# Second layer norm's output and expert weights transposed through block transposes and a DRAM scratch, with three more pipeline stages and a reordered set-up

## The chip, the cores and the metric

The kernel runs on one core of one Trainium2 chip. The metric is the device time of one execution in microseconds (us), from the first to the last instruction. One core has five engines with instruction streams of their own: TensorE (PE; its weight loads are shown apart as PEld), VectorE (DVE), ScalarE (ACT), GpSimd (POOL) and SyncE (SP, which here only starts DMAs). They meet in semaphores. Everything is float32.

## What is computed

The input is 8 sequences of 2048 rows of 256 numbers. Two sublayers, each with a layer norm ahead, a layer norm behind and a residual sum:

```python
x = x + _layernorm(attn(_layernorm(x)))
x = x + _layernorm(ffn(_layernorm(x)))
```

The attention is causal and linear, in chunks of 128 rows, with a running state of 256x256 per sequence. The feed-forward part is the sum of a dense branch and a sparse one that picks 8 of 1024 experts for each of 4 heads:

```python
q = jnp.einsum('btd,ed->bte', hidden_states, W_q)
sim = jnp.einsum('pbthn,hkpn->pbthk', q, keys)
scores_xy, idx_xy = jax.lax.top_k(sim, K)
...
scores, pk = jax.lax.top_k(all_scores, K)
...
w = jax.nn.silu(jnp.einsum('btd,bthkd->bthk', hidden_states, de) * jax.nn.softmax(scores, axis=-1))
experts_states = jnp.einsum('bthk,bthkd->btd', w, ue)
dense = jnp.einsum('bti,di->btd', jax.nn.silu(jnp.einsum('btd,id->bti', hidden_states, W_up)), W_down)
return dense + experts_states
```

## The kernel before

The 16384 rows are 128 tiles of 128 rows, taken chunk by chunk with the 8 sequences in turn, so that tile t follows tile t-8 of its sequence. The kernel is written engine by engine. Each engine has a function `body(t, steady)`, and `pipeline(body)` calls it once per step; `t[k]` is the tile that entered k steps ago. A step handles several tiles at once, each at another stage (`STAGES = 10`). The order of the calls in a body is the order of the engine's instructions, written out by hand. Engines do not share a step's start: they wait for each other only by semaphores.

Gathering nothing, the kernel computes the experts densely: all 1024 products with `down_embed` (`deT`, in two halves of 512), a selection by threshold, and a product of 1024 expert weights with `up_embed` (`ue`).

One tile passes through these steps.

- DVE computes the first norm `xn1`. PE turns it (`turn`, two 128x128 transposes into PSUM), ACT copies it to `xn1T`, and PE forms v, q and k. ACT applies relu and exp to q and k, DVE joins them to `sig`. PE forms the masked scores, the memory product, the numerator and the state update (`ds_ps`, added to `state` by DVE). The result is `mix`, and after another norm `x_mid`.
- DVE computes the second norm `xn2` (line 765). PE turns it (line 587), ACT copies it out of PSUM into `xn2T` (line 639), laid out as [128, 2 buffers, 2 chunks, 128], each chunk contiguous. `xn2T[:, b, c, :]` is the stationary operand of the route product (`sc_ps`) and of the products with `deT` (`d_ps`), and the moving operand of the products with `wupT` (`u_ps`, 128 columns at a time).
- ACT copies the route scores (line 653). POOL adds them pairwise to `sums` for each head (`key_sums`, 128x1024). DVE finds the best eight, POOL forms candidates, DVE selects (`picked`), ACT takes the exponential (`prob`, lines 680 to 709), DVE multiplies, ACT applies Silu into `wexp` (lines 646 to 667).
- Two DMAs issued by POOL (lines 435 and 452) add the four heads of `wexp` together. DVE then transposes the 128x1024 sum in blocks of 32x32 (line 783). Its output pattern `turned_blocks` writes neighbouring elements 8 floats apart. SP stores the result to the DRAM scratch `w_way` (line 375) and reads it back by four DMAs into `gT`, [128, 2, 128, 8] (line 377), which finishes the transposition.
- PE multiplies `gT[:, b, :, c]` as the stationary operand, whose columns lie 8 floats apart, with `ue[:, c, :]` (line 584). The dense branch adds `hT` times `wdownT` into the same bank (line 557). After the last norm DVE forms `x_out`, and SP stores it.

The stationary reads that matter here:

```python
product(y_ps, IC, lambda c: hT[:, t[7] % 2, c, :], lambda c: wdownT[:, c, :], stop=False)
product(y_ps, EC, lambda c: gT[:, t[7] % 2, :, c], lambda c: ue[:, c, :], start=False)
```

In the set-up all weights are loaded by SP, transposed by PE in groups of four blocks (`turned`), evicted by ACT, and centred by DVE (`centre`). PE waits for all of it (`SET_ALL`, `CENT_ALL`) before its first step.

## Time and profile before

| | |
|---|---|
| median of 3 runs | 3030.0 us (3028.74 to 3034.31) |
| the profiled execution, its own time | 3034.47 us |
| its span, first to last instruction | 3032.7 us |
| mean granted TensorE clock | 0.992 |
| busy: PE, PEld | 2970.0 us, 2431.6 us |
| busy: DVE, ACT, POOL | 2420.2 us, 2532.4 us, 1955.8 us |

Busy time counts the compute instructions of an engine. A product in float32 shows as two matmul instructions in the trace, each with a weight load. The duration of a matmul in the trace contains its way through the array, so that neighbours overlap: what a matmul costs its engine is the distance from one start to the next, and this document reads blocks of matmuls from start to start. The same holds to a lesser degree of ACT and DVE, where neighbours overlap by some 0.1 us.

### The profile page before, as it was taken

The page shows a single profiled execution, that of the slowest core. Times are in us where ns is not written, and L with a number is a line of the kernel's source. Part 1 is how long each engine was busy: PE and PEld are TensorE (multiplying, and loading weights), DVE is VectorE, ACT ScalarE, POOL GpSimd, SP SyncE. Part 2 cuts the span into 40 slices and gives each one's busy share as a digit, 9 for nine tenths or more (in the row PEclk, how much of TensorE's full clock was granted, in tenths as well). Part 3 has the DMA queues.
Part 4 walks back from the last instruction along what each step waited for, and adds up shares of the span by engine and source line. Part 5 has one row for each costly group of instructions (what it writes and reads, how often), then busy time and mean ns, then how long its engine had stood idle before and what let it go on. Part 6 is the DMA issues. An engine that isn't in the chain of part 4 may idle for free.

```text
span 3032.7 us, 46880 instructions
## 1 busy us (share of the span) xinstructions
PE 2970.0 (98%) x15402; PEld 2431.6 (80%) x15402; DVE 2420.2 (80%) x5764; ACT 2532.4 (84%) x3854; POOL 1955.8 (64%) x2455
## 2 busy tenths in 40 slices
PE   6899999999999999999999999999999999999996
PEld 5678888888887888888888888888878888888875
DVE  3878888888887888888888788888878888888884
ACT  3888888888888888888888888888888888888884
POOL 2666666666666666666666666666666666666763
PEclk8999999999999999999999999999999999999998
DMA  3455555555555555555555555555555555555555
GB/s 96 96 130 128 122 126 129 125 125 127 129 124 129 127 126 124 127 126 124 131 129 124 122 131 123 129 126 128 124 129 127 125 124 128 125 124 130 129 124 120
DMA packets 188360, 378.33 MB, mean 125 GB/s; under 512 B 18899, under 2 KB 122324, under 8 KB 188116
## 3 DMA queue, kind: packets, MB, share of 16 engines
q0 software_dynamic: 53248, 201.34, 36.9%
q1 hardware_dynamic: 134868, 173.99, 18.3%
q8 instruction: 122, 2.00, 0.3%
q14 instruction: 122, 1.00, 0.1%
HBM read 90.05 MB, written 83.89 MB: 57 GB/s over the span
## 4 chain that ended last, share of the span: by engine, by line
PE 95%; DMA 2%; issue 1%; DVE 1%; POOL 1%; ACT 1%; SPq 0%; POOLq 0%; DVEq 0%
PE banks L529 86%; PE banks L547 3%; PE banks L534 2%; PE banks L608 2%; PE banks L601 1%; DMA wexp<-wexp 1%; DMA sums<-in_L_ffn_keys_dram 0%; SPq L353 0%; POOL sums L418 0%; DMA gT<-w_way 0%; DVE w_blocks L783 0%; PE banks L513 0%; POOL rstd L404 0%; PE banks L520 0%; PE banks L498 0%
## 5 line engine op out<-in xcount | busy, mean ns | idle before, releaser
L418 POOL TENSOR_TENSOR sums<-scores 128x1024 f32<-128x1024 f32 x512 | 1033.9, 2019 | 749.7 <-ACT scores L653 749.7
L404 POOL TENSOR_TENSOR rstd<-var_eps,minus_half 128x1 f32<-128x1 f32 x512 | 498.0, 1110 | 69.0 <-DVE var_eps L855 35.7
L529 PE MATMUL banks<-ue,gT 128*128 128x256 f32 x2048 | 528.9, 412 | 13.7 <-DMA gT<-w_way 13.7
L529 PEld LDWEIGHTS banks<-ue,gT 128*128 128x128 f32 x2048 | 502.7, 336 | 16.1 <-DMA gT<-w_way 14.5
L529 PE MATMUL banks<-xn2T,wupT 128*128 128x128 f32 x4096 | 498.8, 275 | 3.1 <-DVE state L821 3.1
L529 PEld LDWEIGHTS banks<-xn2T,wupT 128*128 128x128 f32 x4096 | 487.4, 192 | 10.1 <-DVE state L821 3.6
L529 PE MATMUL banks<-deT,xn2T 128*128 128x512 f32 x1024 | 481.3, 592 | 0.0
L529 PE MATMUL banks<-wdownT,hT 128*128 128x256 f32 x2048 | 465.0, 380 | 6.0 <-ACT y_sb L650 6.0
L529 PEld LDWEIGHTS banks<-wdownT,hT 128*128 128x128 f32 x2048 | 380.5, 191 | 54.2 <-issue 7.5
L529 PEld LDWEIGHTS banks<-deT,xn2T 128*128 128x128 f32 x1024 | 185.1, 190 | 130.8 <-issue 123.4
L783 DVE STREAM_TRANSPOSE w_blocks<-wexp 128x1024 f32<-128x1024 f32 x128 | 260.9, 2039 | 4.8 <-DMA wexp<-wexp 4.6
L529 PE MATMUL banks<-route,xn2T 128*128 128x512 f32 x512 | 243.5, 598 | 4.6 <-ACT xn2T L639 4.6
L811 DVE SCALAR_TENSOR_TENSOR picked<-sums,cand_best,banks 128x1024 f32<-128x1024 f32 x128 | 163.9, 1280 | 85.2 <-PE banks L529 85.0
L695 ACT ACTIVATE hT<-banks 128x512 f32<-128x512 f32 x128 | 76.4, 597 | 148.1 <-PE banks L529 148.1
L758 DVE SCALAR_TENSOR_TENSOR picked<-sums,cand_best,banks 128x1024 f32<-128x1024 f32 x128 | 163.9, 1280 | 35.5 <-POOL sums L418 35.5
L831 DVE SCALAR_TENSOR_TENSOR prob<-picked,rz,prob 128x1024 f32<-128x1024 f32 x128 | 191.2, 1494 | 0.0
L444 POOL TENSOR_TENSOR cprob<-cmask,cdif 128x112 f32<-128x112 f32 x128 | 59.2, 462 | 199.7 <-DVE cmask L842 199.7
L796 DVE TENSOR_SCALAR dens<-banks 128x2 f32<-128x2 f32 x128 | 20.5, 160 | 204.2 <-PE banks L608 204.2
L787 DVE MAX8 top<-scores 128x8 f32<-128x16 f32 x512 | 83.6, 163 | 116.5 <-ACT scores L653 116.2
L435 POOL DMA_DIRECT2D wexp<-wexp x128 | 158.4, 1237 | 27.9 <-issue 7.4
L695 ACT ACT_TABLE_LOAD x128 | 164.2, 1283 | 2.3
L635 ACT ACT_TABLE_LOAD x128 | 164.2, 1283 | 2.3
(135 smaller groups left out, 6695.9 us busy)
## 6 DMA issues: line engine op xcount, KB each, us to landing
wexp<-wexp POOLq DMA_DIRECT2D x128, 1024.0 KB, 8.0
wexp<-wexp POOLq DMA_DIRECT2D x128, 512.0 KB, 4.6
w_way<-w_blocks SPq DMA_DIRECT2D x128, 512.0 KB, 2.6
gT<-w_way SPq DMA_DIRECT2D x512, 128.0 KB, 3.0
x_in<-_attn_hidden_states_dram SPq DMA_DIRECT2D x128, 128.0 KB, 2.9
out_dram<-x_out SPq DMA_DIRECT2D x128, 128.0 KB, 1.7
wexp<-in_L_ffn_W_up_dram SPq DMA_DIRECT2D x1, 1024.0 KB, 8.3
prob<-in_L_ffn_down_embed_dram SPq DMA_DIRECT2D x1, 1024.0 KB, 10.9
```

The lines of the kernel that those rows point to most:

```text
L404: return nc.gpsimd.tensor_tensor(rstd[:, n, m:m + 1], var_eps[:, n, m:m + 1], minus_half[:, :], ALU.pow)
L418: return nc.gpsimd.tensor_tensor(sums[:, k, :, :], scores[:, k, 0:XIN].unsqueeze(2).broadcast_to([P, XIN, NKEYS]), scores[:, HEADS + k, :] ...
L435: pool.dma_start(wexp[:, 1::2, :], wexp[:, 0::2, :], accum_op=ALU.add).then_inc(s_head_pairs_summed, 16)
L529: last = nc.tensor.matmul(out, lhs(c), rhs(c), start=(start and c == 0), stop=(stop and c == chunks - 1))
L547: last = nc.tensor.matmul(ds_ps[:, c, :], sk_nat[:, c * P:(c + 1) * P], v_one[:, :], start=True, stop=True)
L635: nc.scalar.activation(z_last[:, :], z_last[:, :], ACT.Silu, scale=last_down[:, t[6] % 2:t[6] % 2 + 1], accum_out=w_last[:, t[6] % 2:t[6] ...
L695: nc.scalar.activation(flat(hT[:, t[5] % 2, 4:8, :]), u_ps[1][:, :], ACT.Silu).then_inc(s_hidden_1_ready, 1)
L758: nc.vector.scalar_tensor_tensor(picked[:, 0, :], head(sums, 2), best[:, 2, TOP - 1:TOP], down, ALU.is_ge, ALU.mult).then_inc(s_head_2_sel ...
L783: nc.vector.transpose(turned_blocks(w_blocks, EC), blocks(wexp[:, HEADS - 1, :])).then_inc(s_expert_weights_blocks_turned, 1)
L787: nc.vector.max(top[:, 0, k, :], scores[:, k, 0:XIN])
L811: nc.vector.scalar_tensor_tensor(picked[:, 0, :], head(sums, 0), best[:, 0, TOP - 1:TOP], down, ALU.is_ge, ALU.mult).then_inc(s_head_0_sel ...
L831: nc.vector.scalar_tensor_tensor(prob[:, 0, :], picked[:, 0, :], rz[:, t[5] % 2, 0:1], prob[:, 0, :], ALU.mult, ALU.mult).then_inc(s_head_ ...
```

## The change

- `xn2T` gets the layout [128, 2 buffers, 128, 2 chunks]. PE and ACT no longer make it. DVE transposes `xn2` in blocks of 32x32 into `xn2_blocks`, SP stores that to a DRAM scratch `xn2_way` and reads it back by four DMAs. PE then reads `xn2T[:, b, :, c]`, neighbouring elements 2 floats apart, as stationary operand (route, `deT`) and as moving operand (`wupT`).
- DVE writes `w_blocks` contiguously. The four DMAs read it back into `g_parts`, and a new ACT instruction copies `g_parts` into `gT`, now [128, 2, 8, 128], with contiguous stationary operands.
- `STAGES` goes from 10 to 13. The y products run on `t[10]` rather than `t[7]`, the products with `xn2T` on `t[7]` and `t[6]` rather than `t[5]` and `t[4]`. `hT` gets three buffers, `x_mid` ten slots. The bodies of all engines are written in another order.
- In the set-up, x of tile 0, the keys and `W_rq` are loaded ahead of `ue`, `de_in` and `wdown_in`. The transposes of `down_embed` and `W_down` (`LATE`, 8 groups) are moved into PE's and ACT's first attention step. Centring `ue` and `wdownT` is moved into DVE's steps.

The core of the diff:

```diff
-        xn2T = sb("xn2T", [P, 2, DC, P])
+        xn2T = sb("xn2T", [P, 2, P, DC])
...
+        xn2_blocks = sb("xn2_blocks", [P, D])
+        xn2_way = nc.dram_tensor("xn2_way", [2, P, D], fp32).ap()
...
-        gT = sb("gT", [P, 2, P, EC])
+        gT = sb("gT", [P, 2, EC, P])
+        g_parts = sb("g_parts", [P, BLOCKS, EC, BLOCK])
...
-        STAGES = 10
+        STAGES = 13
...
+            sp.dma_start(x_in[:, 0, :], x_tiles[:, chunk_of(0), seq_of(0), :]).then_inc(s_x_loaded, 16)
+            sp.dma_start(wup_in[:, :, :], W_up.rearrange("(c p) n -> p c n", p=P)).then_inc(s_w_up, 16)
+            sp.dma_start(keys_in[:, :, :, :], keys.rearrange("h k s n -> k h s n")).then_inc(s_w_route, 16)
...
+                if t[9] is not None:
+                    sp.wait_ge(s_expert_weights_blocks_turned, t[9] + 1)
+                    sp.dma_start(w_way[t[9] % 2, :, :], w_blocks[:, :]).then_inc(s_expert_weights_blocks_out[t[9] % 2], 16)
...
+                if t[6] is not None:
+                    sp.wait_ge(s_xn2_blocks_turned, t[6] + 1)
+                    sp.dma_start(xn2_way[t[6] % 2, :, :], xn2_blocks[:, :]).then_inc(s_xn2_blocks_out[t[6] % 2], 16)
...
+                    gather(xn2T[:, t[6] % 2, :, :].rearrange('p (i t) c -> p i (t c)', t=BLOCK), xn2_way[t[6] % 2, :, :], s_xn2_blocks_in[t[6] % 2])
...
-                    turn(t_ps, xn2).then_inc(s_xn2T_in_psum, 1)
...
+                    if t[5] == 0:
+                        late(range(len(parts)))
...
+                    moved(pe, s_xn2_blocks_in, t[6], BLOCKS)
+                    product(sc_ps[:, :], DC, lambda c: xn2T[:, t[6] % 2, :, c], lambda c: route[:, c, :]).then_inc(s_route_scores_in_psum, 1)
...
+                    pe.wait_ge(s_expert_weights_T_ready, t[10] + 1)
+                    product(y_ps, EC, lambda c: gT[:, t[10] % 2, c, :], lambda c: ue[:, c, :], start=False).then_inc(s_y_in_psum, 1)
...
-                    nc.scalar.copy(flat(xn2T[:, t[5] % 2, :, :]), t_ps).then_inc(s_xn2T_ready, 1)
...
+                    nc.scalar.copy(gT[:, t[10] % 2, :, :].rearrange("p c (i t) -> p i c t", t=BLOCK), g_parts[:, :, :, :]).then_inc(s_expert_weights_T_ready, 1)
...
-                    nc.vector.transpose(turned_blocks(w_blocks, EC), blocks(wexp[:, HEADS - 1, :])).then_inc(s_expert_weights_blocks_turned, 1)
+                    nc.vector.transpose(w_blocks[:, :], blocks(wexp[:, HEADS - 1, :])).then_inc(s_expert_weights_blocks_turned, 1)
```

Where the instructions of a steady step stand. First PE, around the expert product and the route product. Before:

```order
L529 MATMUL banks<-xn2T,wupT 128x128 x8
L529 MATMUL banks<-ue,gT 128x256 [waits expert_weights_blocks_in_1]
L529 MATMUL banks<-ue,gT 128x256 x7
L534 MATMUL banks<-ident,xn 128x128 [waits xn2_ready]
L534 MATMUL banks<-ident,xn 128x128
L529 MATMUL banks<-state,sig 128x258 [waits sigma_ready]
L529 MATMUL banks<-state,sig 128x258
L529 MATMUL banks<-route,xn2T 128x512 [waits xn2T_ready]
L529 MATMUL banks<-route,xn2T 128x512
```

And PE now:

```order
L559 MATMUL banks<-xn2T,wupT 128x128 [waits state_ready]
L559 MATMUL banks<-xn2T,wupT 128x128 x7
L559 MATMUL banks<-route,xn2T 128x512 [waits xn2_blocks_in_1]
L559 MATMUL banks<-route,xn2T 128x512
L559 MATMUL banks<-xn1T,wqT 128x128 [waits hidden_1_ready,xn1T_ready]
L559 MATMUL banks<-xn1T,wqT 128x128 x3
L559 MATMUL banks<-xn1T,wkT 128x128 x4
L559 MATMUL banks<-ue,gT 128x256 [waits expert_weights_T_ready]
L559 MATMUL banks<-ue,gT 128x256 x7
L559 MATMUL banks<-xn2T,wupT 128x128 x8
```

The turn of `xn2` is gone, the route product waits for a DMA instead of for ACT, and q and k stand between it and the expert product, which waits for ACT instead of for a DMA.

ACT now, from the last Silu of a step to the copy of `xn1T` in the next (a number of these rows stood in the same order before; the copy of `xn2T` stood behind `z_last`):

```order
L747 ACTIVATE hT<-banks 128x512 [waits up_0_in_psum]
L752 COPY y_sb<-banks 128x256 [waits y_in_psum]
L677 ACTIVATE z_last,w_last<-z_last,last_down 128x112 [waits last_down_ready,last_expert_in_ready]
L681 COPY v_one<-banks 128x256 [waits v_in_psum]
L684 COPY gT<-g_parts 128x4x8x32 [waits expert_weights_blocks_in_1]
L687 ACTIVATE wexp<-prob 128x1024 [waits head_2_weighed]
L693 COPY sk_nat<-banks 128x256 [waits sk_in_psum]
L697 ACTIVATE wexp<-prob 128x1024 [waits head_1_weighed,heads_summed]
L700 ACTIVATE wexp<-prob 128x1024 [waits expert_weights_blocks_turned,head_3_weighed]
L703 ACTIVATE mix<-banks,rden 128x256 [waits denominators_inverted]
```

The new copy of `gT` stands ahead of three Silus and of the `mix` copy on which PE's state update waits.

SP now, one step (`xn_way`, `xn_blocks` stand for `xn2_way`, `xn2_blocks`):

```order
L378 DMA w_way<-w_blocks 128x1024 [waits expert_weights_blocks_turned]
L381 DMA out_dram<-x_out 128x256 [waits x_out_ready]
L384 DMA xn_way<-xn_blocks 128x256 [waits xn2_blocks_turned]
L372 DMA g_parts<-w_way 32x4x256 [waits expert_weights_blocks_out_1,expert_weights_T_ready]
L372 DMA g_parts<-w_way 32x4x256 x3
L372 DMA xn2T<-xn_way 32x4x64 [waits xn2_blocks_out_0]
L372 DMA xn2T<-xn_way 32x4x64 x3
```

Before, a step had the store of `x_out`, the store of `w_blocks`, its four reads and the load of x. Now the reads of `xn2T` stand behind the landing of the `w_blocks` store and behind its four reads.

## Rows read from the trace of the kernel before

**Rows 1.** Page: busy time, share and instructions of each engine.
```profile
PE 2970.0 (98%) x15402; PEld 2431.6 (80%) x15402; DVE 2420.2 (80%) x5764; ACT 2532.4 (84%) x3854; POOL 1955.8 (64%) x2455
```
**Rows 2.** Busy time in stretches: engines, then granted clock, DMA share, GB/s.
```profile
200.00:2900.00 2700.00, 2700.00 (x14085) 2215.87 (x14084) 2209.39 (x5285) 2314.69 (x3523) 1795.06 (x2237) 1.00 0.57 127
...
1504.15:1527.16 23.01, 23.01 (x122) 18.89 (x121) 18.74 (x46) 19.70 (x31) 15.27 (x20) 1.00 0.57 126
```
**Rows 3.** Timeline of PE, middle: start, duration, engine, line, operation, shapes, count.
```profile
1500.91 1.95 PE L529 MATMUL banks<-xn2T,wupT 128*128 128x128 f32 x16
1502.69 4.10 PE L529 MATMUL banks<-ue,gT 128*128 128x256 f32 x16
1506.63 0.38 PE L534 MATMUL banks<-ident,xn 128*128 128x128 f32 x2
1506.85 1.04 PE L529 MATMUL banks<-state,sig 128*128 128x258 f32 x4
...
1515.94 3.62 PE L529 MATMUL banks<-wdownT,hT 128*128 128x256 f32 x16
1519.39 1.95 PE L529 MATMUL banks<-xn2T,wupT 128*128 128x128 f32 x16
...
1523.92 1.95 PE L529 MATMUL banks<-xn2T,wupT 128*128 128x128 f32 x16
```
**Rows 4.** Timeline of PE, first step and first three route products.
```profile
39.92 0.41 PE L534 MATMUL banks<-ident,xn 128*128 128x128 f32 x2 [0.72 <-issue]
...
60.43 2.98 PE L529 MATMUL banks<-route,xn2T 128*128 128x512 f32 x4 [0.55 <-ACT xn2T L639]
...
104.33 1.96 PE L529 MATMUL banks<-route,xn2T 128*128 128x512 f32 x4 [0.55 <-ACT xn2T L639]
```
**Rows 5.** Timeline of the end: last route product, last tile's first adding DMA.
```profile
2971.41 1.98 PE L529 MATMUL banks<-route,xn2T 128*128 128x512 f32 x4 [0.46 <-ACT xn2T L639]
...
2997.14 1.24 POOL L435 DMA_DIRECT2D wexp<-wexp  x1 [3.91 <-ACT wexp L667]
```
**Rows 6.** Groups by shape, PE and weight loads: busy us, mean ns, idle before.
```profile
L529 PE MATMUL banks<-ue,gT 128*128 128x256 f32 x2048 | 528.9, 412 | 13.7 <-DMA gT<-w_way 13.7
L529 PEld LDWEIGHTS banks<-ue,gT 128*128 128x128 f32 x2048 | 502.7, 336 | 16.1 <-DMA gT<-w_way 14.5
...
L529 PEld LDWEIGHTS banks<-wdownT,hT 128*128 128x128 f32 x2048 | 380.5, 191 | 54.2 <-issue 7.5
```
**Rows 7.** Groups by shape, the other engines.
```profile
L418 POOL TENSOR_TENSOR sums<-scores 128x1024 f32<-128x1024 f32 x512 | 1033.9, 2019 | 749.7 <-ACT scores L653 749.7
...
L783 DVE STREAM_TRANSPOSE w_blocks<-wexp 128x1024 f32<-128x1024 f32 x128 | 260.9, 2039 | 4.8 <-DMA wexp<-wexp 4.6
...
L701 ACT ACT_TABLE_LOAD x128 | 164.2, 1283 | 2.3
...
L680 ACT ACTIVATE prob<-sums,neg_max 128x1024 f32<-128x1024 f32 x128 | 147.2, 1150 | 0.6 <-issue 0.2
...
L656 ACT ACTIVATE wexp<-prob 128x1024 f32<-128x1024 f32 x128 | 135.7, 1060 | 0.1
...
L695 ACT ACTIVATE hT<-banks 128x512 f32<-128x512 f32 x128 | 76.4, 597 | 148.1 <-PE banks L529 148.1
```
**Rows 8.** DMA issues: count, KB each, median us from issue to landing.
```profile
w_way<-w_blocks SPq DMA_DIRECT2D x128, 512.0 KB, 2.6
gT<-w_way SPq DMA_DIRECT2D x512, 128.0 KB, 3.0
```
**Rows 9.** Timeline of SP, middle: the four reads of gT in one step.
```profile
1511.98 1.74 SPq L363 DMA_DIRECT2D gT<-w_way  x4
```
**Rows 10.** Timeline of PE, set-up: in brackets the idle time before.
```profile
12.90 2.17 PE L498 MATMUL banks<-ident,wexp 128*128 128x128 f32 x16
...
25.12 3.68 PE L498 MATMUL banks<-ident,wexp 128*128 128x128 f32 x16 [7.77 <-DMA sums<-in_L_ffn_keys_dram]
...
29.72 5.77 PE L513 MATMUL banks<-sums 128*128 128x256 f32 x16
```

More of the change, by code:

```diff
@@ L595, in body @@
-                if t[3] is not None:
-                    product(at_ps, DC, lambda c: sig[:, t[3] % 2, DC + c, :], lambda c: sig[:, t[3] % 2, c, :]).then_inc(s_scores_in_psum, 1)
-                    wait(pe, s_hidden_0_ready, t[3] - 1)
-                    product(mem_ps, DC, lambda c: sig[:, t[3] % 2, c, :], lambda c: mem_x[:, c, :]).then_inc(s_mem_in_psum, 1)
-                    if t[3] < KEPT:
-                        for c in range(DC):
-                            last = nc.tensor.transpose(sk_ps[:, c * P:(c + 1) * P], sig[:, t[3] % 2, DC + c, :], ident[:, :])
-                        last.then_inc(s_sk_in_psum, 1)
@@ L603, in body @@
-                if t[4] is not None:
-                    product(d_ps[1], DC, lambda c: xn2T[:, t[4] % 2, c, :], lambda c: deT[:, c, HALF:]).then_inc(s_down_1_in_psum, 1)
-                if t[3] is not None:
-                    pe.wait_ge(s_v_ready, t[3] + 1)
-                    pe.wait_ge(s_scores_masked, t[3] + 1)
-                    nc.tensor.matmul(num_ps, at[:, :], v_one[:, :], start=t[3] < BATCH, stop=True).then_inc(s_num_in_psum, 1)
+                    product(v_ps, DC, lambda c: xn1T[:, c, :], lambda c: wvo[:, c, :]).then_inc(s_v_in_psum, 1)
@@ L610, in _ @@
+                if t[6] is not None:
+                    wait(pe, s_head_2_selected, t[6])
+                    product(d_ps[1], DC, lambda c: xn2T[:, t[6] % 2, :, c], lambda c: deT[:, c, HALF:]).then_inc(s_down_1_in_psum, 1)
             pipeline(body)
@@ L685, in body @@
-                if t[5] is not None:
-                    act.wait_ge(s_head_1_sums_ready, t[5] + 1)
-                    if not steady:
-                        wait(act, s_head_1_weights_ready, t[5])
-                    nc.scalar.activation(prob[:, 1, :], head(sums, 1), ACT.Exp, bias=neg_max[:, t[5] % 2, 1:2]).then_inc(s_head_1_prob_ready, 1)
-                if t[3] is not None:
-                    act.wait_ge(s_xn1T_in_psum, t[3] + 1)
-                    nc.scalar.copy(flat(xn1T), t_ps).then_inc(s_xn1T_ready, 1)
@@ new lines, in body @@
+                if t[5] is not None:
+                    if t[5] == 0:
+                        late(range(len(parts)))
+                    wait(act, s_sk_in_psum, t[5] + 1, KEPT)
+                    if t[5] < KEPT:
+                        nc.scalar.copy(sk_nat[:, :], sk_ps).then_inc(s_sk_ready, 1)
+                if t[8] is not None:
+                    wait(act, s_heads_summed, 16 * t[8])
+                    act.wait_ge(s_head_1_weighed, t[8] + 1)
+                    nc.scalar.activation(wexp[:, 1, :], prob[:, 1, :], ACT.Silu).then_inc(s_head_1_weights_ready, 1)
+                    act.wait_ge(s_head_3_weighed, t[8] + 1)
+                    wait(act, s_expert_weights_blocks_turned, t[8])
+                    nc.scalar.activation(wexp[:, 3, :], prob[:, 3, :], ACT.Silu).then_inc(s_head_3_weights_ready, 1)
@@ new lines, in body @@
+                if t[5] is not None:
+                    act.wait_ge(s_mix_ready, t[5] + 1)
+                    nc.scalar.activation(mix_sq[:, :], mix[:, :], ACT.Square, scale=D ** -0.5,
+                                         accum_out=var_eps[:, LN_O, t[5] % 2:t[5] % 2 + 1]).then_inc(s_mix_var_eps, 1)
+                    if t[5] == 0:
+                        late(range(len(parts), len(LATE)))
+                if t[7] is not None:
+                    act.wait_ge(s_up_1_in_psum, t[7] + 1)
+                    nc.scalar.activation(flat(hT[:, t[7] % 3, 4:8, :]), u_ps[1][:, :], ACT.Silu).then_inc(s_hidden_1_ready, 1)
+                    act.wait_ge(s_head_3_sums_ready, t[7] + 1)
+                    nc.scalar.activation(prob[:, 3, :], head(sums, 3), ACT.Exp, bias=neg_max[:, t[7] % 2, 3:4]).then_inc(s_head_3_prob_ready, 1)
@@ new lines, in body @@
+                if t[7] is not None:
+                    act.wait_ge(s_head_2_sums_ready, t[7] + 1)
+                    nc.scalar.activation(prob[:, 2, :], head(sums, 2), ACT.Exp, bias=neg_max[:, t[7] % 2, 2:3]).then_inc(s_head_2_prob_ready, 1)
+                    wait(act, s_head_pairs_summed, 16 * t[7])
+                    act.wait_ge(s_head_0_weighed, t[7] + 1)
+                    nc.scalar.activation(wexp[:, 0, :], prob[:, 0, :], ACT.Silu).then_inc(s_head_0_weights_ready, 1)
+                    act.wait_ge(s_up_0_in_psum, t[7] + 1)
+                    nc.scalar.activation(flat(hT[:, t[7] % 3, 0:4, :]), u_ps[0][:, :], ACT.Silu).then_inc(s_hidden_0_ready, 1)
@@ L780, in body @@
[L780 to L785 removed]
+                    dve.wait_ge(s_exp_qk_ready, t[5] + 1)
+                    nc.vector.scalar_tensor_tensor(sig[:, t[5] % 2, :, :], eqk, 1.0, rqk[:, :, :], ALU.min, ALU.add).then_inc(s_sigma_ready, 1)
```

564 lines of the change are left out of this document (291 added, 273 removed).

## The prediction

> **What bounds the kernel now.** The page first: PE is busy for 2970 of 3032.7 us, POOL least [rows 1]. The busy time in stretches says where the missing 63 us are: from 200 to 2900 us PE is busy without a gap at the full granted clock (2.4 GHz), while ACT and DVE are at 86% and 82% [rows 2]. So in the middle nothing but PE's own work counts, and the idle times of the others cost nothing. The timeline of PE gives that work's size: the same block of `wupT` products starts at 1500.91 and 1523.92, a period of **23.01 us** [rows 3]. The rest is ends: PE reaches the first step at 39.92 and the first route product at 60.43 us [rows 4], and from the last route product, at 2971.41, the tail takes 61.3 us [rows 5]. Between those two products lie 127 periods, 2911.0 us or 22.92 each. The profiled execution took 3034.47 us, 1.8 more than its span and 4.5 more than the median; I sum against the span and take the difference off the median.
>
> **The expert product, contiguous.** Its 16 matmuls take 1506.63 - 1502.69 = 3.94 us, 246 ns each; the 16 of the same width with `hT` take 1519.39 - 1515.94 = 3.45, 216 ns each [rows 3]. Why shows in the weight loads: 336 ns where columns lie 8 floats apart, 191 ns where they touch [rows 6], 145 more for 128 columns. If the contiguous one moves 128 columns in about the 111 ns that one load and matmul of the `wupT` product take (1.78/16) [rows 3], the strided one needs some 250 ns, which is just the 246 ns pitch: the load is the bound there. Contiguous, the block becomes a twin of the `hT` block: **-0.49 us per tile**.
>
> **The turn of `xn2`.** Two transposes from 1506.63 to 1506.85: **-0.22 us per tile** [rows 3]. No PE work is added in a steady step. 23.01 - 0.71 = **22.30 us**.
>
> **Reading `xn2T` with stride two.** No row has such a read. As stationary operand it stands before matmuls of 512 columns, at least 427 ns apart (twice the 216 ns of 256 columns), so even the 250 ns load of stride eight would hide: 0. As moving operand it is in 32 matmuls per tile. Lower end: no change, 0 (a gain has no reason). Upper end: as slow as stride eight, 246 instead of 111 ns, 32 x 0.135 = +4.3 us. Between them, if a stride-eight element costs 250/128 = 1.95 ns because each sits in a unit of storage of its own, and two floats share one at stride two, an element costs 0.98 ns, 125 ns per matmul: +0.4 us per tile. I take 0, because the contiguous pitch of 111 ns holds both a load and a stream and shows no more than 14 ns to lose, and keep the other two as rivals. The Trainium skill ("SBUF — State Buffer", the note on cachelines under Door 1) says that accesses run at full bandwidth when at least two hit one 16-byte line. By that rule stride eight pays and stride two does not; the weight loads agree for stride eight (336 against 191 ns), and no row here tests two.
>
> **DVE.** The added transposition is a quarter of the elements of line 783's 2039 ns, so about 0.5 us; line 783 itself, now writing contiguously, takes between 1.06 (an ACT pass over the same size) and 2.04 us [rows 7]. DVE's 18.7 us per step [rows 2] become 18.2 to 19.2, of 22.3. Off the path.
>
> **ACT.** The copy of `xn2T` (256 wide, under the 0.6 us of 512) goes, the copy of `gT` comes: 1.06 us as for a Silu pass over 1024, at most 2.04 [rows 7]. 19.7 us per step become 20.3 to 21.4. Its cover is thin: PE's state update waits for the `mix` copy, and ahead of that ACT now has, from the end of the `wupT` block that feeds `hT`: Silu 0.6, `y_sb`, `z_last` and `v_one` about 1.2 together, `gT` 1.06, three Silus 3.1, `sk_nat` 0.3, `mix` 0.5, 6.7 us, less 0.1 of overlap each, about 6.0. PE in that time, at 216 ns per 256 columns, does v 0.87, `deT` 1.72, then 2.85 of attention, 1.72 of `deT` and a turn 0.22: 7.4 us. So 1.4 us are spare, and 0.4 at the price of 2.04.
>
> **The others' loop.** In the first steps, without y products, two steps still take (104.33 - 60.43)/2 = 21.95 us [rows 4]: the other engines had a loop hardly shorter than PE. The new one goes from POOL's key sums over candidates and `neg_max` to ACT's exponentials and back through `z_last`: four table loads 5.1, four exponentials 4.6, one Silu 1.1, five passes of 512 at 0.6, four small ones 1.8, so 15.6 on ACT; on POOL two key sums 4.0, candidates 1.0, the issue of the adding DMA 0.8 to 1.2, small ones 0.4, so 6.4 [rows 7]. 22.0 end to end, near 20.6 with the overlaps. PE at 22.30 stays the bound by 0.3 to 1.7 us.
>
> **The round trip of `xn2T`.** SP now waits for `w_blocks`, for its landing (2.6), issues four reads (1.7), four more for `xn2T` (1.7) and they land 3.0 later [rows 8, 9]. From route product to route product: q, k and route on PE 3.8, three ACT passes 1.8, `sig` 0.7, DVE up to line 783's twin 3.5, that itself 1.1 to 2.0, SP 9.0: 19.9 to 20.8 us. It stays below 22.30 by 1.5 to 2.4. A quarter of a megabyte per tile is added for DMA engines that are busy 57% of the time [rows 2]. Against the change speaks the Trainium skill ("DMA: Bandwidth & Descriptors", Specifications): transfers under 512 bytes miss line rate, and these pieces have 256. If each piece took twice as long to land, 6.0 for 3.0, the trip would be 23 to 24 us and decide; the pieces are a quarter of the size, though, and no row prices them.
>
> **The ends.** In the set-up PE idles 7.77 us for loads that are now late ones, and its 3.68 us of `wdownT` transposes and 2 us of `deT` transposes move into the first step [rows 10]. PE's set-up becomes: transposes to 15.1, `wvo` and `mem_x` 3.5 to 5.8, keys and route about 4.8; first step near 24 instead of 39.9. In exchange the way to the first route product grows: 20.5 us before, plus 6 for the late transposes, plus 1 for their evictions, plus 6.5 for the DMA trip instead of 1.0 through ACT: 33. First route product at 57 (50 to 66), **-3.4**. Then 127 x 22.30 = 2832.1 instead of 2911.0, **-78.9** (the first steps were light before and are now, so I take the saving against the 22.92). Tail: the last tile's exponentials stand behind more Silus and the copy, some 4.3 us, and the copy of `gT` 1.1, less 1 at line 783: 61.3 + 4.4 = 65.7, **+4.4** (25.7 us of the tail lie ahead of the last tile's first adding DMA, which waits for ACT [rows 5]). Sum of the span: 57 + 2832.1 + 65.7 = 2954.8, 77.9 less. Against the median: 3030.0 - 77.9 = **2952 us**.
>
> **The rivals.**
>
> A (forecast): PE alone is the bound at 22.3 us: 2952, with the ends 2935 to 2968. For it: all loops come out shorter. Chance 0.57.
>
> B: the moving read of stride two costs 1.95/2 ns per element: +0.4 x 128 = +51, 3003. For it: 1.95 ns per strided element; against it: the whole cost would have to fall on the stream. Chance 0.14. The rule of shared lines in the Trainium skill would give A instead.
>
> C: a loop takes over at 22.5 to 22.9 us (POOL and ACT, or the trip of `xn2T`, or the `gT` copy near 2 us): +0.2 to 0.6 us, 2978 to 3028, the likeliest near 2985. For it: margins of 0.3 to 1.7 us of sums made of means; against it: each was summed without overlap first. Chance 0.21.
>
> D (slower): the moving read of stride two is as slow as the stationary read of stride eight. +4.3 x 128 = +553, about 3505. It decides from 130 ns per matmul on, where 32 times the excess over 111 eats the 0.61 us per tile (77.9/128) that A brings. Against it: two floats lie four times closer than eight. Chance 0.05.
>
> E: the change does not do what it says: the expert product stays at 246 ns because something other than the stride sets it. +0.49 x 128 = +63, 3015. Against it: the `hT` twin. Chance 0.03.
>
> **How the numbers follow.** The likeliest is A, 2952. A and B hold 0.71, and the half of C up to 3008 brings it to 0.82, so the range is 2932 to 3008; it leaves out D, E and the upper end of C. Faster by over 0.2% (about what a measurement of this kernel can tell from no change, 6 us): A, B, E and nearly all of C, 0.92; within 0.2% 0.02, from C's end; slower 0.06, from D and C.
>
> **What would show it.** In the profile after: the `ue` block in 3.45 us and its weight loads at 191 ns; the `wupT` blocks at 1.78 us (1.98 would be B, 3.9 D); PE busy without a gap and a period of 22.30 us; where the period is longer, the wait named before route (trip), `ds_ps` (`gT` copy) or q and k (POOL and ACT loop) says which part of C it is. The first step should start near 24 us, the first route product near 57. The prediction fails if some row of PE waits in every step, or if the `wupT` blocks grow.

## The result: slower, and where the time is

| | before | after |
|---|---|---|
| median | 3029.4 us (3028.5 to 3034.3, 4 runs) | 3087.8 us (3080.1 to 3097.9, 4 runs) |
| ratio to before | | 1.0191 (1.0154 to 1.0229) |
| profiled execution, its span | 3034.5, 3032.7 us | 3094.1, 3092.3 us |

The changed kernel is 1.9% slower. The prediction had said 2952 us and gave slower a chance of 0.06.

First the busy times of the page after, and the stretch from 200 to 2900 us (columns as in [rows 1] and [rows 2]):

```profile
PE 2922.4 (95%) x15146; PEld 2343.3 (76%) x15146; DVE 2373.6 (77%) x5892; ACT 2592.2 (84%) x3854; POOL 2040.8 (66%) x2455
```
```profile
200.00:2900.00 2700.00, 2603.58 (x13614) 2094.65 (x13613) 2131.57 (x5315) 2329.67 (x3466) 1836.47 (x2196) 1.00 0.59 136
```

PE has less to do, 48 us less in all, but where it was busy without a gap before [rows 2] it now stands still for 96 of 2700 us. The mean granted clock rounds to 1.00 there, though single steps fall below it (further down). No engine is busier in that stretch than PE, so the time goes in waiting. For what, the groups say (busy us, mean ns of one, then idle before and its releaser):

```profile
L559 PE MATMUL banks<-ue,gT 128*128 128x256 f32 x2048 | 464.5, 380 | 0.3 <-ACT gT L684 0.3
L559 PEld LDWEIGHTS banks<-ue,gT 128*128 128x128 f32 x2048 | 380.6, 191 | 48.9 <-issue 1.5
L559 PE MATMUL banks<-route,xn2T 128*128 128x512 f32 x512 | 263.9, 640 | 119.7 <-DMA xn2T<-xn_way 119.3
```

The first two answer to [rows 6]: the strided expert product is cured, 191 ns for 336 per weight load, and it waits for nothing. The third is new: **119 us of waiting at the route product, for the reads of `xn2T`**. The view of waits splits it (us in total, times, longest):

```profile
PE banks L559 <- DMA xn2T<-xn_way: 119.3, 85, 4.2
```

So the wait comes in some 85 of 128 steps, and up to 4 us long. PE's timeline in the middle (start, duration, then idle before and what ended it) shows a step with it and one without:

```profile
1483.94 3.11 PE L559 MATMUL banks<-route,xn2T 128*128 128x512 f32 x4 [2.47 <-DMA xn2T<-xn_way]
...
1501.63 0.38 PE L564 MATMUL banks<-ident,xn 128*128 128x128 f32 x2
...
1506.18 1.98 PE L559 MATMUL banks<-xn2T,wupT 128*128 128x128 f32 x16
1507.99 1.88 PE L559 MATMUL banks<-route,xn2T 128*128 128x512 f32 x4
...
1511.50 3.62 PE L559 MATMUL banks<-ue,gT 128*128 128x256 f32 x16
1514.95 1.98 PE L559 MATMUL banks<-xn2T,wupT 128*128 128x128 f32 x16
...
1523.91 0.38 PE L564 MATMUL banks<-ident,xn 128*128 128x128 f32 x2
...
1531.60 0.71 PE L559 MATMUL banks<-route,xn2T 128*128 128x512 f32 x1 [1.17 <-DMA xn2T<-xn_way]
```

From 1501.63 to 1523.91 no wait falls, and the period is **22.28 us**, the forecast 22.30 almost to the digit. But the route products at 1483.94, 1507.99 and 1531.60 lie 24.05 and 23.61 us apart. Over the whole run the first is at 53.32 and the last at 3024.90: 23.40 us per step. That is 1.10 us above the forecast 22.30, times 127 it is 140 us, and it accounts for the miss (137.5 us of span: 3092.3 against 2954.8).

Why the data is late stands in the chain of work that ended last (start, duration, what). Its path between two route products, of which the lines of DVE are the last two ahead of the store:

```profile
1531.60 3.79 PE banks L559 x20
...
1540.41 0.35 DVE xn_blocks L836
1540.77 1.14 DVE w_blocks L841
1541.92 2.67 DMA w_way<-w_blocks
...
1548.23 7.19 DMA xn2T<-xn_way
...
1555.47 3.79 PE banks L559 x20
```

This is the round trip of `xn2T` of the prediction, step for step, and it takes 23.87 us. Without the last landing it takes 16.68. The landing takes 7.19 us; the prediction put 3.0 there.

Much of the run has another pattern: one step with the wait, the next without. There the same chain spans two steps:

```profile
1579.27 11.62 PE banks L559 x60
...
1618.01 7.25 DMA xn2T<-xn_way
...
1625.30 11.62 PE banks L559 x60
```

It goes over PE's products up to the turn of `xn1`, then over ACT's exponentials, POOL's `cprob` and key sums, DVE's products, and then the same store and reads. It takes 46.03 us, 38.78 without the landing. What PE needs for two steps is 2 x 22.28 = 44.56. So a landing of some 5.6 us in the one loop and 5.8 us in the other is free, and one of 7 is not.

Some waits cost more than their idle time. After the 2.47 us ahead of the route product at 1483.94 the granted clock (the column behind POOL's) is below full:

```profile
1483.94:1486.84 2.90, 2.90 (x5) 1.18 (x5) 2.48 (x7) 0.62 (x1) 2.90 (x4) 0.63 0.10 20
1486.84:1489.22 2.38, 2.38 (x17) 2.38 (x16) 0.00 (x0) 0.00 (x0) 0.74 (x2) 0.74 1.03 196
```

Of its two levels, 1.2 and 2.4 GHz, part of this stretch ran at the lower one: route, q and k took 5.28 us where they take 3.51 after no wait, 1.8 us more. After the 2.52 us of waiting ahead of 1458.92 the clock stayed at 1.00. Between 200 and 2800 us five steps show such a loss, some 9 us in all, so the waits themselves are by far the larger part.

What else moves when the reads are issued is in the timelines of SP and POOL, here ahead of the route product at 1531.60:

```profile
1518.67 0.34 SPq L378 DMA_DIRECT2D w_way<-w_blocks  x1
...
1521.43 1.74 SPq L372 DMA_DIRECT2D g_parts<-w_way  x4
1523.22 1.86 SPq L372 DMA_DIRECT2D xn2T<-xn_way  x4
```
```profile
1523.17 1.22 POOL L488 DMA_DIRECT2D wexp<-wexp  x1
```

POOL starts its first adding DMA, 1 MB, in the very microsecond in which the reads of `xn2T` begin. This is so in nearly every step: in 123 of 128 it starts between 0.7 us before and 0.9 us after the first of these reads. The DMA rows of the page (KB each, median us from issue to landing) show who suffers, and the last line, from the view of the tile `xn2T`, its spread:

```profile
wexp<-wexp POOLq DMA_DIRECT2D x128, 1024.0 KB, 8.3
...
x_in<-_attn_hidden_states_dram SPq DMA_DIRECT2D x128, 128.0 KB, 6.9
...
xn2T<-xn_way SPq DMA_DIRECT2D x512, 32.0 KB, 2.7
```
```profile
DMA to landing us min/median/max: 1.7/2.7/8.8
```

The median over all reads looks harmless. It is the last of the four on which PE waits, and that one is issued deepest into the adding DMA. It lands at 1531.56, and the adding DMA, issued at 1523.17 with a landing of 8.3, ends at about 1531.5: the small read comes home with the large transfer. The load of x, issued behind it, does the same, 6.9 us.

### The profile page after: what moved, and what is told of

It reads as the page before. It is cut to its first block, busy times and chain, and to the rows that moved or that the text cites. A ratio compares the mean times of both kernels' runs of the same rounds, so it can differ in the third digit from the quotient of the medians.

```text
span 3092.3 us, 47586 instructions
## 1 busy us (share of the span) xinstructions
PE 2922.4 (95%) x15146; PEld 2343.3 (76%) x15146; DVE 2373.6 (77%) x5892; ACT 2592.2 (84%) x3854; POOL 2040.8 (66%) x2455
## 3 DMA queue, kind: packets, MB, share of 16 engines
q0 software_dynamic: 53248, 201.34, 34.7%
q1 hardware_dynamic: 227028, 207.59, 22.3%
q8 instruction: 121, 1.98, 0.3%
q14 instruction: 129, 1.06, 0.1%
## 4 chain that ended last, share of the span: by engine, by line
DMA 28%; PE 28%; DVE 12%; ACT 9%; SPq 8%; issue 8%; POOL 6%; DVEq 0%; POOLq 0%; ACTq 0%
PE banks L559 26%; DMA xn2T<-xn_way 20%; SPq L372 8%; DMA w_way<-w_blocks 7%; DVE w_blocks L841 3%; DVE prob L832 3%; POOL sums L438 3%; DVE prob L824 2%; POOL cprob L455 2%; POOL rstd L424 2%; ACT L714 2%; ACT prob L714 1%; DVE picked L816 1%; ACT prob L718 1%; DMA wexp<-wexp 1%
## 5 line engine op out<-in xcount | busy, mean ns | idle before, releaser
L424 POOL TENSOR_TENSOR rstd<-var_eps,minus_half 128x1 f32<-128x1 f32 x512 | 463.2, 976 | 257.2 <-ACT mix_sq L721 209.9
L559 PE MATMUL banks<-ue,gT 128*128 128x256 f32 x2048 | 464.5, 380 | 0.3 <-ACT gT L684 0.3
L473 POOL TENSOR_TENSOR wexp<-wexp,w_last 128x1 f32<-128x1 f32 x128 | 24.3, 190 | 651.6 <-ACT z_last L677 651.6
L559 PEld LDWEIGHTS banks<-ue,gT 128*128 128x128 f32 x2048 | 380.6, 191 | 48.9 <-issue 1.5
L559 PE MATMUL banks<-route,xn2T 128*128 128x512 f32 x512 | 263.9, 640 | 119.7 <-DMA xn2T<-xn_way 119.3
L732 ACT ACTIVATE rqk<-banks 128x512 f32<-128x512 f32 x128 | 76.6, 598 | 208.6 <-PE banks L559 208.6
L455 POOL TENSOR_TENSOR cprob<-cmask,cdif 128x112 f32<-128x112 f32 x128 | 170.7, 1334 | 114.0 <-DVE cmask L921 114.0
L559 PEld LDWEIGHTS banks<-route,xn2T 128*128 128x128 f32 x512 | 92.9, 201 | 200.3 <-DMA xn2T<-xn_way 136.0
L820 DVE SCALAR_TENSOR_TENSOR sig<-banks,rqk 128x512 f32<-128x512 f32 x128 | 88.5, 691 | 149.4 <-ACT banks L739 149.4
L559 PEld LDWEIGHTS banks<-xn1T,wqT 128*128 128x128 f32 x1024 | 141.5, 201 | 67.5 <-issue 66.5
L914 DVE SCALAR_TENSOR_TENSOR prob<-picked,rz,prob 128x1024 f32<-128x1024 f32 x128 | 164.4, 1285 | 17.4 <-DVE rz L910 0.5
```

The lines of the kernel that those rows point to most:

```text
L424: return nc.gpsimd.tensor_tensor(rstd[:, n, m:m + 1], var_eps[:, n, m:m + 1], minus_half[:, :], ALU.pow)
L455: nc.gpsimd.tensor_tensor(cprob[:, :, :], cmask[:, :, :], cdif[:, :, 0:NCAND], ALU.mult).then_inc(s_cand_prob_ready, 1)
L559: last = nc.tensor.matmul(out, lhs(c), rhs(c), start=(start and c == 0), stop=(stop and c == chunks - 1))
L820: nc.vector.scalar_tensor_tensor(sig[:, t[5] % 2, :, :], eqk, 1.0, rqk[:, :, :], ALU.min, ALU.add).then_inc(s_sigma_ready, 1)
L914: nc.vector.scalar_tensor_tensor(prob[:, 1, :], picked[:, 1, :], rz[:, t[7] % 2, 1:2], prob[:, 1, :], ALU.mult, ALU.mult).then_inc(s_head_ ...
```

## The experiments

Three theories can explain the 119 us. **T**: the reads meet the adding DMA on the DMA engines. **S**: pieces of 256 bytes are slow by themselves. **O** (later with P): the new order of the engines' work, and the place of the reads in SP's row, make the loop too long whatever the DMA engines do. Two more runs price the strided read, on which rivals B and D rested.

### e1: the small transfer first

```diff
+                if t[6] is not None:
+                    sp.wait_ge(s_xn2_blocks_turned, t[6] + 1)
+                    sp.dma_start(xn2_way[t[6] % 2, :, :], xn2_blocks[:, :]).then_inc(s_xn2_blocks_out[t[6] % 2], 16)
                 if t[9] is not None:
                     sp.wait_ge(s_expert_weights_blocks_turned, t[9] + 1)
                     sp.dma_start(w_way[t[9] % 2, :, :], w_blocks[:, :]).then_inc(s_expert_weights_blocks_out[t[9] % 2], 16)
...
+                if t[6] is not None:
+                    moved(sp, s_xn2_blocks_out, t[6], 1)
+                    wait(sp, s_up_0_in_psum, t[6] - 1)
+                    gather(xn2T[:, t[6] % 2, :, :].rearrange('p (i t) c -> p i (t c)', t=BLOCK), xn2_way[t[6] % 2, :, :], s_xn2_blocks_in[t[6] % 2])
                 if t[9] is not None:
...
                     gather(g_parts[:, :, :, :].rearrange("p i c t -> p i (c t)"), w_way[t[9] % 2, :, :], s_expert_weights_blocks_in[t[9] % 2])
-                if t[6] is not None:
...
-                    gather(xn2T[:, t[6] % 2, :, :].rearrange('p (i t) c -> p i (t c)', t=BLOCK), xn2_way[t[6] % 2, :, :], s_xn2_blocks_in[t[6] % 2])
```

> Edit: in SP's step the store of xn2_blocks, then (behind the stores of w_blocks and x_out) the four reads of xn2T stand ahead of the four reads of g_parts, so the reads of xn2T are issued some 3 us earlier, ahead of POOL's 1 MB adding DMA. Theory T (the reads of xn2T land 7 to 8 us after their issue because they share the DMA engines with the adding DMA, 2.7 us otherwise, and this closes a loop of two steps): the route product no longer waits, PE's period is 22.38 us throughout, the span near 53 + 127 x 22.38 + 67 = 2963, time about 2960 to 2975. Theory S (pieces of 256 bytes are slow by themselves): the last read of xn2T still lands some 7 us after its issue, but earlier by 3 us in all, so the waits shrink to few; time 2965 to 3000; the landing time tells it from T. Theory O (the new order of POOL, DVE and ACT is the bound, and the wait for xn2T is only where it shows): the wait moves to another row, time stays above 3060.

Measured: **2942.6 us** (2939.8 to 2944.3, 4 runs), ratio to before 0.9725 (0.971 to 0.9739). The period is 22.27 us. SP's timeline, the group of the route product and the landing of the reads:

```profile
1511.35 0.34 SPq L378 DMA_DIRECT2D xn_way<-xn_blocks  x1
1512.48 0.32 SPq L381 DMA_DIRECT2D w_way<-w_blocks  x1
...
1513.37 2.23 SPq L372 DMA_DIRECT2D xn2T<-xn_way  x4
1515.70 1.81 SPq L372 DMA_DIRECT2D g_parts<-w_way  x4
```
```profile
L558 PE MATMUL banks<-route,xn2T 128*128 128x512 f32 x512 | 243.6, 598 | 1.1 <-DMA xn2T<-xn_way 1.1
```
```profile
DMA to landing us min/median/max: 1.6/1.9/3.1
```

The wait is gone: 1.1 us for 119.7. The same 256-byte pieces, as many of them, land in 1.9 us and never later than 3.1, so S falls. The adding DMA still takes 8.4 us, but it is issued at 1517.27, when the reads of `xn2T` are in. This version beats both kernels. It also lies below theory T's 2960 to 2975: that sum had 22.38 us for each of 127 steps, and they take 22.18 on average (from 55.46 to 2872.03), because the first and the last few are lighter. It moves two things at once, though: the reads leave the adding DMA, and the loop becomes shorter by the store and the four reads ahead. (In both e1 and e5, SP's wait for PE's earlier `wupT` products, left out of the steady steps before, is made in every step.) The next runs part the two.

### e2: half the bytes added

The kernel leaves half of the expert weights of heads 0 and 2 out of the sum.

```diff
-                    pool.dma_start(wexp[:, 1::2, :], wexp[:, 0::2, :], accum_op=ALU.add).then_inc(s_head_pairs_summed, 16)
+                    pool.dma_start(wexp[:, 1::2, 0:HALF], wexp[:, 0::2, 0:HALF], accum_op=ALU.add).then_inc(s_head_pairs_summed, 16)
```

> Edit: the changed kernel with POOL's first adding DMA over 512 of the 1024 columns, so that half of the expert weights of heads 0 and 2 are not added (that part of the sum is left out). All orders and issues stay. Theory T: the adding DMA is over in half the time, the reads of xn2T land 3 to 5 us after issue instead of 7 to 8, the route product hardly waits, time 2965 to 2990. Theory S: the landing is as in the changed kernel and so is the time, 3080 to 3098. Theory O: time as in the changed kernel, with the wait gone from the route row.

Measured: 2946.3 us in one run, period 22.27 us. The DMA rows and the wait:

```profile
wexp<-wexp POOLq DMA_DIRECT2D x256, 512.0 KB, 5.4
```
```profile
L559 PE MATMUL banks<-route,xn2T 128*128 128x512 f32 x512 | 245.0, 601 | 12.1 <-DMA xn2T<-xn_way 12.0
```

SP's order is untouched; the reads begin at 1517.76 and the adding DMA at 1518.03, so they still meet. The longest landing is 6.2 us for 8.8, and the wait falls from 119.3 to 12.0 us. That is T's result, with a time below its 2965 to 2990. The neighbour's length sets the delay: in this step the last of the four reads, issued at 1519.2, takes 4.5 us to land, and the adding DMA issued at 1518.03 takes 5.4, so both end near 1523.5. That is less than the loops have to spare (5.6 and 5.8). This is the cleanest of the tests: bytes alone are changed, so no theory of order or place explains it.

### e3: the turn back on PE

`xn2` is turned by PE and copied by ACT again, as before, within the new order and stages. The reads of `xn2T` don't exist.

```diff
-        xn2T = sb("xn2T", [P, 2, P, DC])
+        xn2T = sb("xn2T", [P, 2, DC, P])
...
+                    turn(t_ps, xn2).then_inc(s_xn2T_in_psum, 1)
...
-                    moved(pe, s_xn2_blocks_in, t[6], BLOCKS)
+                    pe.wait_ge(s_xn2T_ready, t[6] + 1)
...
+                    nc.scalar.copy(flat(xn2T[:, t[6] % 2, :, :]), t_ps).then_inc(s_xn2T_ready, 1)
```

> Edit: the changed kernel without the DMA trip of xn2: PE turns xn2 between the hT products and the wupT products, ACT copies it to xn2T with contiguous chunks ahead of its Silu for hT, as in the kernel before; all the rest, 13 stages, the new orders, the contiguous gT and the set-up, stays. Theories T and S: PE's two transposes come back, 22.30 + 0.22 = 22.5 us per tile and no wait, time 2965 to 2990. Theory O: the period stays at 23.4 on average, time above 3060.

Measured: 2962.0 us (2959.8 to 2963.9), ratio 0.979 (0.9773 to 0.9806), period 22.44 us.

```profile
200.00:2850.00 2650.00, 2649.57 (x14152) 2134.43 (x14151) 2138.38 (x5312) 2424.11 (x3660) 1889.75 (x2247) 1.00 0.58 130
```

From 200 to 2850 us PE is busy without a gap. So the new order of PE, ACT, DVE and POOL, the longer `gT` copy on ACT and the three added stages are no bound, and O falls as far as it speaks of them (DVE's transposition of `xn2`, 0.44 us, is gone here too). It also prices the DMA trip when nothing disturbs it: e1's 22.27 against 22.44, 0.17 us per step, the 0.22 of the turn less what reading with stride two costs.

### e4: only the contiguous expert weights

The kernel before with contiguous `w_blocks`, `g_parts`, the ACT copy and contiguous `gT`; its stages, its order and its set-up stay.

```diff
-        gT = sb("gT", [P, 2, P, EC])
+        gT = sb("gT", [P, 2, EC, P])
+        g_parts = sb("g_parts", [P, BLOCKS, EC, BLOCK])
...
-                    product(y_ps, EC, lambda c: gT[:, t[7] % 2, :, c]
+                    product(y_ps, EC, lambda c: gT[:, t[7] % 2, c, :]
...
+                    nc.scalar.copy(gT[:, t[7] % 2, :, :].rearrange("p c (i t) -> p i c t", t=BLOCK), g_parts[:, :, :, :]).then_inc(s_expert_weights_T_ready, 1)
...
-                    nc.vector.transpose(turned_blocks(w_blocks, EC), blocks(wexp
+                    nc.vector.transpose(w_blocks[:, :], blocks(wexp
```

> Edit: the kernel before with one part of the change: w_blocks written contiguously, read back into g_parts, copied by ACT into a contiguous gT, the copy placed where ACT waits for the wupT products anyway. All theories: the expert product takes 3.45 instead of 3.94 us, 0.49 us per tile or 63 us in all less, time 2965 to 2972, if the other engines' loop, seen at 21.95 us in the first steps, is really below 22.5 us.

Measured: 2973.5 us (2971.7 to 2978.5), ratio 0.9831 (0.9816 to 0.9845), period 22.53 us for 23.01. The expert product alone brings 0.48 us per tile; the prediction had 0.49. The time is 1.5 us above the 2965 to 2972 expected. Most of e1's gain is here: 52 us of 83, both against the same seven runs of the kernel before (3025.2 us).

### e5 and e6: place or company

e5 changes the place of the four reads in SP's row, and but for the wait named under e1 nothing else. e6 leaves SP and every byte alone and has POOL start the adding DMA later, behind `neg_max`, `cdif`, the power and the last key sums.

```diff
                 if t[7] is not None:
                     key_sums(3).then_inc(s_head_3_sums_ready, 1)
+                if t[8] is not None:
+                    pool.dma_start(wexp[:, 1::2, :], wexp[:, 0::2, :], accum_op=ALU.add).then_inc(s_head_pairs_summed, 16)
...
                     pool.wait_ge(s_head_3_weights_ready, t[7] + 1)
-                    pool.dma_start(wexp[:, 1::2, :], wexp[:, 0::2, :], accum_op=ALU.add).then_inc(s_head_pairs_summed, 16)
```

> Against the changed kernel one thing is moved: SP issues the four reads of xn2T ahead of the four reads of g_parts, the three stores keep their order. The reads then start when the store of xn2_blocks has landed, some 1.8 us earlier than now, and still in the few microseconds in which POOL's adding DMA of 1 MB is issued. Theory T (the reads of xn2T land late because they meet the adding DMA, and this closes a loop over two steps): a part of PE's waits goes, since most of the reads get ahead of the adding DMA: period 22.3 to 22.8 us, 2950 to 3010 us, landing of the xn2T reads 2 to 4 us in the median. Rival P (their place in SP's row alone makes them late; the adding DMA has no part): 1.8 us earlier in every step is less than the 2.2 us that PE waits in two steps, but landing stays at 2.7 us in the median and up to 8.8 us, and the time lands at 2950 to 2960 us only if every wait goes. The two differ in the longest landing.

> Against the changed kernel one instruction is moved: POOL starts the first adding DMA (1 MB, wexp onto wexp) behind neg_max, cdif, one power and the last key sums instead of ahead of them, some 3.2 us later. SP's order and every byte stay. Theory T (the reads of xn2T meet the adding DMA): the reads, issued at the same moment as now, are through before it starts; PE's waits for xn2T fall from 119 us to under 30 us, the longest landing from 8.8 to under 5 us, period 22.3 to 22.6 us, 2945 to 2985 us. What could eat it: the second adding DMA and the turning of w_blocks come up to 1 us later. Rival P (place in SP's row, and the length of the chain through POOL, ACT and DVE): the reads are issued at the same moment or up to 1 us later, so PE waits as much as now or more: 3080 to 3120 us.

Measured: e5 2943.2 us (2940.0 to 2946.8), ratio 0.9718 (0.9701 to 0.9734); **e6 2943.4 us** (2940.8 to 2944.5), ratio 0.9714 (0.97 to 0.9729). Of e6, SP's and POOL's timelines, the group of the route product and the landing of the reads:

```profile
1512.57 0.34 SPq L378 DMA_DIRECT2D w_way<-w_blocks  x1
...
1517.10 1.87 SPq L372 DMA_DIRECT2D xn2T<-xn_way  x4
```
```profile
1519.85 1.21 POOL L450 DMA_DIRECT2D wexp<-wexp  x1
```
```profile
L560 PE MATMUL banks<-route,xn2T 128*128 128x512 f32 x512 | 245.7, 603 | 5.8 <-DMA xn2T<-xn_way 5.8
```
```profile
DMA to landing us min/median/max: 1.7/2.4/3.6
```

In e6 the reads stand 4.5 us behind the store of `w_blocks`, as in the changed kernel (1523.22 - 1518.67 there, 1517.10 - 1512.57 here), and behind the same four larger reads. Only the adding DMA stands 7.3 us behind that store instead of 4.5. The wait falls to 5.8 us and the kernel is 144 us faster than the changed one, for one moved line. P, which had 3080 to 3120, falls. One thing besides the meeting changes: the issue of the adding DMA, 1.2 us on POOL, no longer stands ahead of `neg_max`, on which ACT's exponentials wait. e2, where it still does, says that this isn't needed for the gain. T's range, 2945 to 2985, was slightly too high here as well.

e5 comes to the same time by a smaller step; theory T had 2950 to 3010 for it and P 2950 to 2960, so the time fits neither range. The landings, by which the two were to be told apart, speak for T in the median and leave single long ones. Of this kernel, the landings of `xn2T` and a DMA row of the page:

```profile
DMA to landing us min/median/max: 1.6/1.8/7.0
```
```profile
g_parts<-w_way SPq DMA_DIRECT2D x512, 128.0 KB, 7.7
```

The reads come out before the adding DMA (issued 1.4 us after them), and now the reads of `g_parts` run into it: 7.7 us to land for 3.0. That costs nothing, since ACT copies them a good part of a step later. It also says again that the size of the pieces isn't it: `g_parts` comes in pieces of 1 KB and is delayed as much. The long landings of single reads of `xn2T` did not vanish, but they fall where no loop waits. The sum of e1, e2, e5 and e6: four different ways to part the reads from the adding DMA, or to shorten it, all end at 2943 to 2946 us.

How the DMA engines share is not tested by any of these runs; that the large transfer's company is the cause, they show. The Trainium skill ("DMA: Bandwidth & Descriptors", Queues, rings and completion order) says that each DMA engine takes turns between the queues that have work, one packet from each. By the page of the changed kernel POOL's queue moved 201.34 MB in 53248 packets, 3.8 KB each, and SP's 207.59 MB in 227028, 0.9 KB each. If these are the packets that the page means, which no run here shows, the queue with small packets would get the smaller part of the bytes while both have work; the reads that land with the end of the adding DMA would fit that.

### s4 and s8: what a strided moving operand costs

Rivals B and D rested on a price that no row had. Here it is measured by itself, in the kernel before: `xn1T` is laid out at a pitch of 4 or 8 floats. It is the moving operand of q and k (16 matmuls of 128 columns) and the stationary one of v.

```diff
-        xn1T = sb("xn1T", [P, DC, P])
+        xn1T = sb("xn1T", [P, P, 4])
...
-                            last = product(qk_ps[:, col:col + P], DC, lambda c: w[:, c, ec * P:(ec + 1) * P], lambda c: xn1T[:, c, :])
+                            last = product(qk_ps[:, col:col + P], DC, lambda c: w[:, c, ec * P:(ec + 1) * P], lambda c: xn1T[:, :, c])
```

> The kernel before with xn1T laid out with its elements 4 floats apart (ACT writes it so, PE reads it as the moving operand of q and k, 16 matmuls of 128 columns per tile, and as the stationary operand of v, 4 per tile). Rate rule (each element of a moving read costs 1.95 ns as soon as two of them no longer share 16 bytes, the size that the weight loads at stride eight gave): 250 ns instead of 111 per matmul, blocks of 8 at 2.0 us instead of 0.89, +2.2 us per tile, about 3320 us. Rival (only weight loads suffer from a stride, moving reads do not): blocks stay at 0.9 us, 3030 to 3045 us.

> The same with the elements 8 floats apart. Rate rule: as for 4, about 3320 us, since an element that sits alone costs the same at any distance. If the cost grows with the distance, blocks of 8 take over 2.0 us here. Rival (moving reads do not suffer): 3030 to 3045 us.

Measured, one run each: 3281.8 us at a pitch of 4, 3297.5 at 8, against 3029.5 before. PE's timeline at a pitch of 4, then at 8:

```profile
1520.66 1.20 PE L529 MATMUL banks<-wvo,xn1T 128*128 128x256 f32 x4
1521.70 2.00 PE L529 MATMUL banks<-xn1T,wqT 128*128 128x128 f32 x8
1523.52 2.02 PE L529 MATMUL banks<-xn1T,wkT 128*128 128x128 f32 x8
1525.36 1.97 PE L529 MATMUL banks<-xn2T,wupT 128*128 128x128 f32 x16
```
```profile
1507.59 2.02 PE L529 MATMUL banks<-xn1T,wqT 128*128 128x128 f32 x8
1509.44 2.04 PE L529 MATMUL banks<-xn1T,wkT 128*128 128x128 f32 x8
```

From start to start a matmul of 128 columns takes 1.82/8 = 228 ns at a pitch of 4 and 1.85/8 = 231 ns at 8. Contiguous it takes 111 (1.78/16, [rows 3]), and at a pitch of 2, in the changed kernel, (1507.99 - 1506.18)/16 = 113 ns. That is a step between 2 and 4, not a slope: 2, 117 and 120 ns more. The rate rule (250 ns) was right in kind and 10% high in size. Moving reads pay for a stride as weight loads do, and the cost doesn't grow from 4 to 8. The sum holds as well: q and k take 1.82 and 1.84 us for 0.98 and 0.89 before, v 1.04 for 0.87, together 1.96 us more per tile or 251 in 128, and 252 were measured.

The Trainium skill's rule ("SBUF — State Buffer", the note on cachelines under Door 1: lines of 16 bytes, full bandwidth from two hits per line on) is borne out: at a pitch of 2 floats two share 16 bytes and cost 2 ns, at 4 none do and they cost 117. The same note of the Trainium skill gives 4 fp32 as how far one can stride for free; read as a pitch, that is not what was measured, and the measured 228 ns for 111 decides.

## Why the prediction was wrong, point by point

**PE as the bound, and its period: right.** Steps without a wait last 22.28 us for a forecast 22.30. The expert product takes 1514.95 - 1511.50 = 3.45 us for 3.45, and e4 confirms it alone (0.48 for 0.49). The turn brought 0.17 net for 0.22 (e1 against e3).

**Stride two: right to take 0.** The `wupT` block before the route product takes 1.81 us for 1.78 (rival B 1.98, D 3.9): 0.07 us per tile where B had 0.4. As stationary operand it costs 197 ns for 190 per weight load (`deT` products), hidden.

**DVE and ACT: right.** From the groups of the changed kernel:

```profile
L841 DVE STREAM_TRANSPOSE w_blocks<-wexp 128x1024 f32<-128x1024 f32 x128 | 154.1, 1204 | 15.0 <-DMA wexp<-wexp 15.0
...
L684 ACT COPY gT<-g_parts 128x1024 f32<-128x1024 f32 x128 | 136.1, 1063 | 4.9 <-DMA g_parts<-w_way 4.7
...
L836 DVE STREAM_TRANSPOSE xn_blocks<-xn 128x256 f32<-128x256 f32 x128 | 56.2, 439 | 0.1
```

1.20 us for 1.06 to 2.04, 1.06 for 1.06, and 0.44 for 0.5. The cover that was called thin held: PE's expert product waits 0.3 us for the `gT` copy in the whole run.

**The round trip of `xn2T`: the step that failed.** "They land 3.0 later" was taken from the landing of `gT` [rows 8], reads that before stood alone. The trip was summed at 19.9 to 20.8 us. With a landing of 3.0 it would have been 16.68 + 3.0 = 19.7; with the real 7.19 it is 23.87. The prediction even had the case, "6.0 for 3.0, the trip would be 23 to 24 us and decide", and dropped it because the pieces are small. It asked what a piece costs, and not what else is on the DMA engines in the microsecond in which SP would issue it. That was a question that the order of the changed kernel raises: POOL may issue the adding DMA only after the Silu that waits for `w_blocks` to be turned (ACT L700), and SP's store, its landing and the reads wait for that same turning. The semaphores set only the earliest moment; in the steps shown this Silu starts some 3 us after the turning without waiting. But the two keep close: the adding DMA stands 4.1 to 5.5 us behind the store in 124 of 128 steps, and the reads 4.5 to 4.9 in the steps shown, so this is no chance meeting.

**The others' loop: below PE, as forecast, but joined to the trip.** It was given 20.6 to 22.0 us, apart from the trip. In the chain the two are joined into one loop over two steps, 38.78 us and a landing. With 3.0 for the landing that is 20.9 us per step, 1.4 below PE, and the trip alone would be 2.6 below. So the room that was forecast (1.5 to 2.4) was there. It was the landing, 4.2 us longer than its term, that used it up in both loops.

**The ends: right in sum.** First route product at 53.3 (57 forecast), tail 67.4 (65.7). The first step came at 27.5 for 24; the 32 small route products of the set-up, 5.2 us, are the largest item on the way. The late transposes took 1.7 and 1.8 us, not 6.

**The middle: its saving was summed too small.** The mean of 22.92 us before already holds the light first and last steps, so the whole 0.71 per step, 90 us, should have come off it, and not 0.62, 78.9 us. e1, whose steady steps have no wait, needs 2816.6 us from the first route product to the last, for 2832.1 forecast. The two errors point in opposite ways: without the waits the kernel is faster than 2952 (e1, 2942.6).

**The rivals.** C named the mechanism ("the trip of `xn2T`") and was priced at no more than 22.9 us per step, where the loop takes 23.40 on average. Its own working held the 23 to 24 us that should have been its upper end; with that the rival would have crossed to the slower side. D, which held nearly all of the chance of slower, was wrong: its price is real (117 ns for 135), but a pitch of 2 doesn't pay it. Slower came out of the rival that was thought to stay faster.

## What to carry to other kernels

A transfer's landing is not a constant of its size: before a DMA goes into a loop, look at what the other queues start in the same microseconds, above all when both hang on the same event, and take for the landing what the row beside such company shows. Issue the small transfer on which the bound engine waits first, or have the large one start a few microseconds later; here one moved line was worth 144 us. Where several loops stay below the bound, sum them joined, over two steps as well (here 20.9 us per step, where the trip alone had 19.7), and give a rival the worst price that its own working names.
